# Spectral layer of a fused conv, attention and expert kernel: the first product in 64x64 blocks, small loads regrouped

## The reference

```python
B, C, H, W = x.shape                       # 4, 192, 16, 16
xr = x.reshape(B, H, W, C)
Xf = jnp.fft.fft2(xr, axes=(1, 2), norm='ortho').reshape(B, H, W, nb, bs)   # nb = 8 blocks of bs = 24 channels
xk = Xf[:, :, :kept]
xr_, xi_ = (xk.real, xk.imag)
o1r = relu(einsum('bhwni,nio->bhwno', xr_, w1[0]) - einsum('bhwni,nio->bhwno', xi_, w1[1]) + b1[0])
o1i = relu(einsum('bhwni,nio->bhwno', xi_, w1[0]) + einsum('bhwni,nio->bhwno', xr_, w1[1]) + b1[1])
o2r = einsum('bhwno,noi->bhwni', o1r, w2[0]) - einsum('bhwno,noi->bhwni', o1i, w2[1]) + b2[0]
o2i = einsum('bhwno,noi->bhwni', o1i, w2[0]) + einsum('bhwno,noi->bhwni', o1r, w2[1]) + b2[1]
o2r, o2i = softshrink(o2r, 0.01), softshrink(o2i, 0.01)
out = irfft2((o2r + 1j * o2i).reshape(B, H, W, C), s=(H, W), axes=(1, 2), norm='ortho').reshape(B, C, H, W) + x
```

## Time and profile before

| what | us |
|---|---|
| median of the three runs | 228.53 |
| the profiled execution's own time | 227.28 |
| its span | 225.4 |
| PE busy in the span | 217.2 |
| DVE busy | 148.7 |
| ACT busy | 113.8 |
| forward transform on PE, as the chain of waits has it | 4.37 |
| first product | 4.08 |
| second product | 4.94 |

### The profile page before, as it was taken

The page is one execution under the profiler, slowest core; times in us unless marked ns, Lnnn a source line. Parts: engine busy times, 40 slices in busy tenths (PEclk is TensorE's granted clock), DMA queues, the critical chain, the costliest instruction groups (busy, mean ns, idle before and its releaser), DMA issues.

```text
span 225.4 us, 5766 instructions
## 1 busy us (share of the span) xinstructions
PE 217.2 (96%) x1975; PEld 140.8 (62%) x1975; DVE 148.7 (66%) x353; ACT 113.8 (50%) x205; POOL 77.2 (34%) x119
## 2 busy tenths in 40 slices
PE   7999999999999999999999999999999999897994
PEld 3988866765676676767755745655556565453393
DVE  3558767677878888787879756666566666560262
ACT  0742274555444444345643567566575766653271
POOL 7040052000001811837101626566565666442100
PEclk9999999999999999999999999999999999999999
DMA  6973564939989979015600211111211111210444
GB/s 179 184 186 88 153 237 102 292 75 354 287 165 292 244 200 286 0 38 171 198 20 0 52 34 52 52 42 52 52 52 48 52 40 52 55 35 22 146 153 140
DMA packets 28115, 27.53 MB, mean 122 GB/s; under 512 B 7804, under 2 KB 26940, under 8 KB 28092
## 3 DMA queue, kind: packets, MB, share of 16 engines
q1 hardware_dynamic: 22444, 21.15, 34.0%
q0 software_dynamic: 2304, 4.72, 7.5%
q10 hardware_dynamic: 3344, 1.36, 2.3%
HBM read 22.34 MB, written 3.44 MB: 114 GB/s over the span
## 4 chain that ended last, share of the span: by engine, by line
PE 88%; DVE 5%; ACT 3%; issue 2%
PE grid L1624 11%; PE bank L1650 10%; PE grid L1365 8%; PE grid L1631 7%; PE bank L1640 4%; PE bank L1385 4%; PE bank L1227 4%; PE grid L1511 3%; PE grid L1335 3%; PE bank L1402 3%; PE bank L1335 2%; PE bank L1287 2%; PE bank L1350 2%; PE grid L1525 2%; PE bank L1193 2%
## 5 line engine op out<-in xcount | busy, mean ns | idle before, releaser
L1110 DVE COPY main<-main 128x1152 f32 x39 | 30.3, 790 | 15.2 <-issue 13.6
L776 ACT ACTIVATE main<-down_all 128x576 f32 x40 | 27.2, 684 | 25.6 <-PE bank L1650 24.7
L742 ACT ACTIVATE main<-grid 128x1024 f32<-128x1024 f32 x23 | 23.6, 1025 | 26.3 <-PE grid L1365 26.3
L589 POOL DMA_INDIRECT main<-xhat_rows,main x21 | 26.9, 1282 | 24.4 <-PE bank L1610 13.4
L597 POOL DMA_INDIRECT pair_rows<-main x19 | 20.2, 1061 | 25.6 <-DVE main L1100 25.6
L1624 PE MATMUL grid<-main 128*64 128x384 f32 x152 | 28.2, 488 | 0.6 <-DVE main L1094 0.6
L1335 PE MATMUL grid<-main 32*128 32x256 f32 x132 | 27.1, 401 | 0.0
L1365 PE MATMUL grid<-main 32*128 32x256 f32 x192 | 26.3, 398 | 0.8 <-ACT main L742 0.6
L913 DVE TENSOR_REDUCE main<-grid 128x2 f32<-128x512 f32 x33 | 21.8, 685 | 4.4 <-PE grid L1335 3.6
L1650 PEld LDWEIGHTS bank<-main 128*64 128x64 f32 x228 | 16.1, 136 | 12.4 <-ACT main L776 8.9
L1650 PE MATMUL bank<-main 128*64 128x192 f32 x228 | 22.7, 333 | 0.0
(11 more groups left out here) (221 smaller groups left out, 395.3 us busy)
## 6 DMA issues: line engine op xcount, KB each, us to landing
down_all<-wd SPq DMA_DIRECT2D x4, 1152.0 KB, 7.0
main<-wg SPq DMA_DIRECT2D x4, 576.0 KB, 4.6
main<-wu SPq DMA_DIRECT2D x4, 576.0 KB, 6.1
main<-wg SPq DMA_DIRECT2D x4, 288.0 KB, 6.8
main<-wu SPq DMA_DIRECT2D x4, 288.0 KB, 8.0
main<-main SPq DMA_DIRECT2D x8, 128.0 KB, 3.6
main<-x SPq DMA_DIRECT2D x1, 768.0 KB, 7.5
main<-wg SPq DMA_DIRECT2D x2, 384.0 KB, 5.7
```

Of the source, the lines that this page charges most:

```text
L589: pool.indirect_dma_start(xg[:, t % 2, :], None, xhat_rows, bass.IndirectOffsetOnAxis(ap=slot_token[:, t:t + 1].bitcast(U32), axis=0)).the ...
L742: act.activation(probs[:, quad % 2, 2 * (n % 2):2 * (n % 2) + 2, :, :].rearrange("p h k n -> p h (k n)"), grid[:, score_banks(n), :], ACT. ...
L776: act.activation(w_dn[:, p, h, :], dn_e(expert(t, h)), ACT.Copy).then_inc(S["w_dn_ready"], 1)
L1110: vec.tensor_copy(w_gu[:, p, h, :], gu_e(expert(t, h))).then_inc(S["w_gu_ready"], 1)
```

## The change

The 4 groups are now read as `k` in 0 and 1 (partition halves) times a slot `q`: block `4k + q` has its real part at partitions `64k` to `64k + 23` and its imaginary part at `64k + 32` to `64k + 55`. The forward transform writes quarters: its statements on line 1194 make 32 output rows by 72 columns, four to different quarters in a row, 128 statements for 64. The first product takes 64x64 blocks: `k` picks the rows of the array and `side` the columns, so the four statements that stand together use its four quadrants, 16 statements for 8. `w1` shrinks to 64 columns a slot. DVE evicts every second result of the first product (line 881), ACT the others (line 659); `negate` needs two instructions of 32 rows each where it had one of 64.

Loads: SP issues all eight of w2 and ACT none, ACT issues four of b1 for two, and no longer waits for five memsets but three. `w_proj` and `b_proj` stand ahead of `w_qkv`, the gate's loads get a semaphore of their own. The wait for `ld_qkv` and the four copies to `w_first` stand behind the addition on line 1002 (before: line 993).

```diff
-        w1 = carve(GROUPS * 128).rearrange("p (q r o) -> p q r o", q=GROUPS, r=2)
+        w1 = carve(GROUPS * 128)[:, 0:GROUPS * 64].rearrange("p (q r o) -> p q r o", q=GROUPS, r=2)
...
+        def load_w1(queue, k):
+            block_k = a["w1"].rearrange("r (k q) i o -> k r i q o", k=2)[k]
             for r in range(2):
-                queue.dma_start(dst[i, :, r, o], block_k[r]).then_inc(sem, 16)
-                queue.dma_start(dst[im, :, 1 - r, o], block_k[r]).then_inc(sem, 16)
+                for imag in range(2):
+                    first = 64 * k + 32 * imag
+                    queue.dma_start(w1[first:first + BLK, :, r ^ imag, 0:BLK], block_k[r]).then_inc(S["ld_w1"], 16)
...
             sp.wait_ge(S["zeroed"], 3)
-            load_blocks(sp, w1, a["w1"], S["ld_w1"], 1)
-            load_blocks(sp, w2, a["w2"], S["ld_w2"], 1)
+            load_w1(sp, 1)
+            for side in range(2):
+                load_w2(sp, side)
...
-            act.wait_ge(S["zeroed"], 5)
-            load_blocks(act, w1, a["w1"], S["ld_w1"], 0)
+            act.wait_ge(S["zeroed"], 3)
+            load_w1(act, 0)
...
-            load_blocks(act, w2, a["w2"], S["ld_w2"], 0)
...
-            act.wait_ge(S["ld_b1"], 2 * 16)
-            for v in range(2 * GROUPS):
-                bp, q = v // GROUPS, v % GROUPS
+            act.wait_ge(S["ld_b1"], 4 * 16)
+            for v in range(0, 2 * GROUPS, 2):
+                bp, q = v // GROUPS, v % GROUPS // 2
                 act.wait_ge(S["hid_done"], v + 1)
                 act.activation(hid[:, q, bp * 2 * MODES:(bp + 1) * 2 * MODES],
                                bank[4 + v % 4][:, 0:2 * MODES], ACT.Relu, bias=b1[:, q:q + 1]).then_inc(S["hid_ready"], 1)
...
-            negate(w2, "ld_w2", 9)
+            dve.wait_ge(S["ld_b1"], 4 * 16)
+            for v in range(1, 2 * GROUPS, 2):
+                bp, q = v // GROUPS, GROUPS // 2 + v % GROUPS // 2
+                if v == GROUPS + 1:
+                    negate(w2, "ld_w2", 9)
+                dve.wait_ge(S["hid_done"], v + 1)
+                vec.tensor_scalar(hid[:, q, bp * 2 * MODES:(bp + 1) * 2 * MODES], bank[4 + v % 4][:, 0:2 * MODES],
+                                  b1[:, q:q + 1], 0.0, ALU.add, ALU.max).then_inc(S["hid_dve"], 1)
...
                     for q in range(2):
-                        col = y * C + (2 * (u % 2) + q) * GC
                         at_mode = q * MODES + y * (MODES // 2)
-                        for r in range(2):
-                            last = mm(bank[u][IM * r:IM * r + IM, at_mode:at_mode + MODES // 2], folded[:, b, col:col + IM],
-                                      fwd[:, y, r, :], start=True, stop=True)
+                        for k in range(2):
+                            col = y * C + (4 * k + 2 * (u % 2) + q) * BLK
+                            for r in range(2):
+                                last = mm(bank[u][64 * k + 32 * r:64 * k + 32 * r + 32, at_mode:at_mode + MODES // 2], folded[:, b, col:col + 32],
+                                          fwd[:, y, r, :], start=True, stop=True)
...
-                mm(bank[4 + v % 4][:, 0:2 * MODES], w1[:, q, :, :], spec[:, q, bp * 2 * MODES:(bp + 1) * 2 * MODES],
-                   start=True, stop=True).then_inc(S["hid_done"], 1)
...
+                    for k, side in ((0, 0), (1, 1), (0, 1), (1, 0)):
+                        last = mm(bank[4 + 2 * v + k][64 * side:64 * side + 64, 0:2 * MODES], w1[64 * k:64 * k + 64, 2 * v + side, :, :],
+                                  spec[64 * k:64 * k + 64, 2 * v + side, bp * 2 * MODES:(bp + 1) * 2 * MODES], start=True, stop=True)
+                        if (k, side) in ((0, 1), (1, 0)):
+                            last.then_inc(S["hid_done"], 1)
...
-            dve.wait_ge(S["ld_qkv"], 16 * 12)
-            dve.wait_ge(S["w_zeroed"], 6)
-            for rows, m, part in ((slice(0, 128), 0, 0), (slice(0, 128), 1, 1), (slice(64, 128), 2, 0), (slice(0, 64), 2, 1)):
-                vec.tensor_copy(w_first[rows, m, :].rearrange("p (x t) -> p x t", t=2)[:, :, 0],
-                                w_d[rows, m, 0, part, :]).then_inc(S["w_spread"], 1)
             dve.wait_ge(S["ld_res"], 16)
...
                     vec.tensor_tensor(bproj_all[:, :], bank[3][:, 0:C], bproj, ALU.add).then_inc(S["out_bias_ready"], 1)
+                    dve.wait_ge(S["ld_qkv"], 16 * 12)
+                    dve.wait_ge(S["w_zeroed"], 6)
+                    for rows, m, part in ((slice(0, 128), 0, 0), (slice(0, 128), 1, 1), (slice(64, 128), 2, 0), (slice(0, 64), 2, 1)):
+                        vec.tensor_copy(w_first[rows, m, :].rearrange("p (x t) -> p x t", t=2)[:, :, 0],
+                                        w_d[rows, m, 0, part, :]).then_inc(S["w_spread"], 1)
```

More of the change, by code:

```diff
@@ L437, in _ @@
                          .rearrange("(q p f) -> p q f", q=2, p=128)).then_inc(S["ld_res"], 16)
+            sp.wait_ge(S["w_zeroed"], 6)
+            for r in range(4):
+                sp.dma_start(wproj[32 * r:32 * r + HD, :, :],
+                             a["w_proj"].rearrange("(j r d) n -> r d j n", r=4, d=HD)[r]).then_inc(S["ld_attn"], 16)
+            sp.dma_start(bproj[:, :], a["b_proj"].partition_broadcast(128)).then_inc(S["ld_attn"], 16)
             for rows, m, start in ((slice(0, 128), 0, 0), (slice(0, 128), 1, C - 128), (slice(64, 128), 2, 128), (slice(0, 64), 2, 0)):
@@ L635, in _ @@
                 load_pixels(act, b)
-            act.wait_ge(S["zeroed"], 5)
-            load_blocks(act, w1, a["w1"], S["ld_w1"], 0)
+            act.wait_ge(S["zeroed"], 3)
+            load_w1(act, 0)
             with nc.allow_non_contiguous_dma(reason="a bias per channel"):
-                for r in range(2):
-                    act.dma_start(b1[IM * r:IM * r + GC, :], a["b1"][r].rearrange("n o -> (n o)").rearrange("(q p) -> p q", p=GC)).then_inc(S["ld_b1"], 16)
-            load_blocks(act, w2, a["w2"], S["ld_w2"], 0)
+                for side in range(2):
+                    for r in range(2):
+                        first = 64 * side + 32 * r
+                        act.dma_start(b1[first:first + BLK, :], a["b1"][r].rearrange("(g s) o -> s o g", s=2)[side]).then_inc(S["ld_b1"], 16)
             for b in range(B):
@@ L857, in negate @@
                 dve.wait_ge(S[loaded], 16 * count)
-                vec.tensor_scalar(w[IM:, :, 0, :], w[IM:, :, 0, :], -1.0, None, ALU.mult).then_inc(S["negated"], 1)
+                for first in (32, 96):
+                    vec.tensor_scalar(w[first:first + 32, :, 0, :], w[first:first + 32, :, 0, :], -1.0, None, ALU.mult).then_inc(S["negated"], 1)
             fold(0)
@@ L1181, in _ @@
                 last.then_inc(S["spec_done"], 1)
[L1183 to L1185 removed]
+            pe.wait_ge(S["negated"], 2)
+            for bp in range(2):
                 pe.wait_ge(S["spec_act"], 2 * (bp + 1))
                 pe.wait_ge(S["spec_dve"], 2 * (bp + 1))
[L1189 to L1194 removed]
@@ L1196, in _ @@
-            pe.wait_ge(S["negated"], 2)
+                for v in range(2):
+                    if bp:
+                        pe.wait_ge(S["hid_ready"], v + 1)
+                        pe.wait_ge(S["hid_dve"], v + 1)
+                    else:
+                        pe.wait_ge(S["spec_act"], B // 2 + v + 1)
+                        pe.wait_ge(S["spec_dve"], B // 2 + v + 1)
+                    for k, side in ((0, 0), (1, 1), (0, 1), (1, 0)):
[3 more added lines that the diff above has]
+                            last.then_inc(S["hid_done"], 1)
@@ L1197, in _ @@
+            pe.wait_ge(S["negated"], 4)
             pe.wait_ge(S["spec_act"], B)
@@ L1200, in _ @@
                 pair, k = u // 3, u % 3
-                pe.wait_ge(S["hid_ready"], GROUPS * (pair + 1))
+                pe.wait_ge(S["hid_ready"], GROUPS // 2 * (pair + 1))
+                pe.wait_ge(S["hid_dve"], GROUPS // 2 * (pair + 1))
                 if u >= 4:
@@ L1393, in project_out @@
                     if b == 0:
[L1394 removed]
+                        pe.wait_ge(S["ld_attn"], 6 * 16)
                     else:
```

56 lines of the change are left out of this document (22 added, 34 removed).

## The result

The changed kernel takes **229.74 us** (median of 20 runs) where the kernel before takes 228.0 (20 runs beside it): a ratio of 1.0072, interval 1.0057 to 1.0088. It is slower by 0.7%; 227.0 was predicted, from a median of before of 228.53 (three runs). The profiled execution took 230.42 us, with a span of 227.7 for the 225.4 of before.

What follows compares the result with a forecast made beforehand. The prediction took PE, busy 217.2 of 225.4 us, as the bound. Its terms, first product −1.5 and all others 0, took the median of 228.53 to 227.0 us, with a range of 226.2 to 229.1.

Steps and rivals of the forecast that it cites:

- The forward transform: Fourier layer's start on PE: 256 matmuls for 128, four at the pace of two, 4.0 us, cost 0.
- such a rate for long: Forward transform: doubt that one load and matmul pair each 0.016 us, seen only in a burst, would last.
- (c): Forward transform: PE's instruction intake holds matmuls 0.031 us apart; +2.0 us in all, 230.6, chance 0.06.
- (d): Forward transform: a floor of 0.025 us a matmul, 6.4 us; +0.5 in all, 229.0, chance 0.12.
- The first product: Product after the forward transform: four quadrants side by side, second product begun at 11.75 instead of 13.22, 1.5 us gained.
- w2, b1, DVE, the rest of SP's queue: Loads and DVE work around the products, later SP loads: hidden, cost 0 each, at most some tenths for DVE and SP.
- rival (a): Before the second product: w2's load becomes the bound, b2 landing past 11.1; gain 0.3 to 1.1, 227.8, chance 0.15.
- Rival (b): After the products: a later gate that does not move with PE takes the gain; gain 0 to 0.4, 228.3, chance 0.12.
- The move of w_first: DVE's wait for w_qkv before PE's tokens: without the move nearly all the gain ends; with it cost 0.
- The sum: Whole kernel: forward 0, first product −1.5, the rest 0; 225.8 against the profiled run, 227.0 against the median.

Runs made afterwards that it cites:

- e1: The kernel before with only the forward statements split, each of 64 rows written as two of 32; 230.39 us, ratio 1.0105.
- e2: The changed kernel with sixteen small matmuls, 32 more instructions, ahead of the forward transform; 228.79 us (one run).
- e4: The changed kernel with the loads of w2 shared between SP and ACT again, four each; 228.49 us, ratio 1.0045.
- e7: The changed kernel with forward statements of 128 columns, 16 for 128, and the first product on 32x64 tiles; 228.25 us, ratio 1.0005.
- e3: The changed kernel with 112 small matmuls ahead of the forward transform and six of the eight long idle ones left out; 229.11 us, ratio 1.006.
- e5: The kernel before with all of the change but the forward transform's quarters and the first product's blocks; 227.73 us, ratio 1.0012.
- e8: The kernel before with forward quarters for images 0 and 1 only, halves for 2 and 3; median 231.26 us, ratio 1.0154.
- e9: e7 with the wait for w_qkv and the four copies to w_first back ahead of the input's additions; median 233.72 us, ratio 1.0175.
- e10: e7 with 16 small matmuls added ahead of PE's warming; 227.26 us, ratio 0.9987.
- e11: e7 with 48 small matmuls added ahead of PE's warming and two of the eight long ones left out; 227.21 us, ratio 0.9964.

## Why the prediction was wrong, step by step

**The forward transform: this step failed.** The prediction took its cost at 0, from bursts, and put its doubt at "such a rate for long". As a sum of matmul time the 0 holds (4.44 us for 4.37; 215 matmuls in 3.56 us are 0.0166 each), and rivals (c) and (d), a floor per matmul of 0.031 or 0.025, fall. Rival (c) was near in kind, since it named PE's intake of instructions, but not as a steady pace: that its 230.6 is close to the profiled 230.42 is chance. The cost came from what no row of it was read for: the list of DMA queues, where the packets of instructions stand. Every stop in the six traces that have one fits. The two counts are of PE's recorded instructions, ahead of the packet's start and ahead of the stop:

```
            packet start  end     PE stops  resumes   start to resume   count at packet  at stop
after       6.90          8.35    8.35      10.37     3.47              295              449
e1          6.66          8.19    8.22      10.08     3.42              279              449
e2          7.20          8.50    8.75      10.63     3.43              281              449
e4          7.52          8.93    8.88      10.43     2.91              303              449
e7          17.27         18.36   19.01     19.89     2.62              412              449
e3 (2nd)    8.37          9.76    10.06     11.27     2.90              523              705
e3 (3rd)    17.06         18.33   19.04     19.72     2.67              915              961
```

Seven stops, in three different stages of the work, lie behind instructions 449, 449 + 256 and 449 + 512, and in the first 25 us of all twelve traces PE stands for half a microsecond or more without a wait nowhere else. Whether PE stops there depends on how long before it the packet started: with a stop, 2.6 to 3.5 us pass from the packet's start to the next instruction; in before, e5, e8, e9, e10 and e11, which don't stop, the 450th instruction is issued 3.9 to 8.9 us after that start. The bound is not sharp: e3 passes its first boundary 3.21 us behind the packet's start, and e2 its second 2.43 us behind, both without a stop. In the five stops of the quarters, PE has 146 to 182 instructions left when the packet starts. An estimate from these: some 165 instructions must last some 3.2 us, 20 ns each. The quarters, at 8.7, cannot make that. Whether the halves, at 17, would make it no run shows: none has the 450th instruction within them (17.02 us in before, 16.56 in e5, 13.71 in e8). What sets the packet's start is open: it lies 0.2 to 5.8 us behind PE's 193rd instruction (449 − 256) in these traces.

The runtime page of the Trainium skill ("Runtime: NRT & Kernel Launch", section "Instruction fetch mechanics") says the instructions come in blocks of 16 KiB, 256 instructions, while the one before is executed, and that this is mostly hidden. The block's size agrees with the packets of 16384 bytes and with the 256 instructions between the stops here. "Mostly hidden" does not hold for the quarters: 2.03, 1.86, 1.88, 1.55 and 1.20 us were not. The same section gives PE room for 2048 instructions, and at another place only for two blocks; a first stop behind 449 and the next 256 later speak for two.

**What the prediction had no term for: the clock.** Behind the stop the granted clock fell to 0.50 in the profiled run (11.71 to 15.12), and the first product took 3.86 us for the 2.82 of e2 and e4. It does not always fall: of the changed kernel's 20 runs 14 had a mean clock of 0.990 to 0.993 and a median near 229.9, six had 0.998 or more and a median near 228.6. So a fall is worth 1.4 us where it comes. It is not the stop's alone: of the 54 runs of before whose clock is on record (those beside the experiments), nine had 0.990 or 0.991 and a median of 228.65, the other 45 one of 227.48, and e7's profiled run has its fall at 113.72 to 117.13, far from its stop; e2, e3 and e4 have the stop and a full clock. So the stop goes with falls more often (14 of 20 for 9 of 54); that it brings them about is likely, not shown, and where the falls of the other 13 runs lie no trace shows. Runs without a fall against such runs of before are 1.1 us longer (228.6 for 227.5, not taken side by side); the stop less the product's gain is 2.03 − 1.26 = 0.8.

**The first product: right in kind, 0.2 short.** Predicted −1.5, measured −1.26 at full clock (2.82 for 4.08). The four sets of four quadrants do run side by side (32 matmuls in 2.82 us, 0.088 each, for 0.255). They take a little more than the 2.6 us allowed for: 1.36, a wait of 0.15, 1.31. DVE's eviction took 0.52 us, where its copy's 0.46 was taken.

**w2, b1, DVE, the rest of SP's queue: right in the outcome.** No DMA wait before the second negation; e5 is within 0.0031 of before. The last of w2's and b2's loads landed at 10.77 in the changed kernel, 10.8 by the prediction, and that is luck: b2 was issued at 8.81 and not at 7.3, behind an issue of 1.96 us, and landed 2.0 us later and not 3.3 or 5.0. In the changed kernel the negation stood 2.6 us later than forecast (13.76 for 11.13), so it tests little; but e7 has all of w2's loads and b2 on SP too and negates at 11.23 without a wait, so rival (a) falls. Rival (b), a gate that takes the gain, had no gain to take in the changed kernel.

**The move of w_first: right, and the size too small.** "Without it nearly all the gain would end here" was the claim; e9 is 2 us or more above e7 even by its lowest run against e7's median (230.64 for 228.25). The wait moved the tokens by 1.4 us (25.07 for 23.70). The rest goes with the low clock behind PE's wait of 2.36 us: 10.25 us of it in the profiled run, which the prediction had no term for either.

**The sum** put 225.8 against the profiled run; it has 230.42. The 4.6 between are the stop 2.03, the first product 3.86 − 2.6 = 1.26, and 0.07 for the transform, which make 3.4 at the second product (15.11 for 11.75). Another 0.2 was lost by the tokens (+2.07 for +1.89). The last 1.0 is not settled: 0.2 of it lies in the rest of the span, and 0.8 around the span, where this execution took 2.7 us and that of before 1.9.

## What to carry to other kernels

Splitting statements so that more tiles run side by side costs instructions even when it costs the array nothing: count them per microsecond as well as per tile. 512 PE instructions in 4.4 us, matmuls and their weight loads counted apart, ran dry here in all five kernels that had them. Fewer instructions are no full protection: e7 stopped in its inverse transform, with 120 in about 5 us, where its packet started late. Where PE stands on "issue" while every engine and queue rests, look for the instruction packets, and count PE's instructions up to the stop: if the stop keeps its count when work is put ahead of it, it is the end of a block. Then wider statements are the first thing to try; small matmuls ahead shift the end of a block to another place in the work, but whether its packet comes in time they don't settle.

## What the runs showed that was not expected

**DMA issues stall beside an instruction block.** Most issues on SP and ACT take 0.4 to 0.6 us. In the twelve traces 68 take 1 us or more; 62 of these overlap a packet on PE's instruction queue, and 55 of the 62 end 0.35 to 0.44 us after that packet does. Five of them:

```
            packet        issue began   took    ended     after the packet
before      9.41-10.32    SP 9.45       1.28    10.72     0.40
before      17.67-18.86   SP 17.56      1.67    19.23     0.37
after       6.90-8.35     SP 6.81       1.96    8.77      0.42
after       12.92-13.84   SP 12.99      1.22    14.21     0.37
e8          36.99-38.46   SP 36.99      1.84    38.83     0.37
```

So an issue that is under way with a block of instructions for PE can be delayed by 0.8 to 1.6 us. Not each is: of the 148 issues that overlap such a packet 86 take under 1 us, many of them begun well ahead of it. What holds them is open. In the changed kernel it cost nothing on the path, and it is part of what e8 lost.

**The clock comes up at a different time in each run.** The first record of a granted clock in the trace lies at 4.88 us in the changed kernel, 5.20 in before, 6.00 in e4, 6.11 in e2, 6.91 in e10, 6.53 in e11, 7.69 in e3. The page reads 1.00 ahead of it as well, but the pace says otherwise. Each transform's first half takes 2.13 us plus half of what lies between its start and that record, as at the level of 1.2 GHz: e3 2.13 + (7.69 − 4.70) / 2 = 3.63 (measured 3.61), e4 2.74 (2.73), e11 3.13 (3.18), before 2.34 (2.37). PE had been kept busy by the same eight long matmuls from 1.2 us on (1.5 in e10) in all but e3 and e11. What sets the moment is open; it shifts a profile by up to 0.9 us (e10, 3.00 for 2.13) in kernels with those eight, so two chains are to be compared from the transform's second half on, and kernels by their medians.
